# The opening and closing steps of a two-layer graph network in another order, with x of pair 3 loaded ahead of the later weights

## The reference

```
def gat_heads(x, adj, W, a):
    Wh = einsum('bnf,hfo->bhno', x, W)
    f1, f2 = Wh @ a[:, :O], Wh @ a[:, O:]
    e = leaky(f1[..., :, None] + f2[..., None, :])
    attn = softmax(where(adj > 0, e, -1e9), axis=-1)
    return einsum('bhnm,bhmo->bhno', attn, Wh)

h = relu(layernorm(x))
h = elu(gat_heads(h, adj, W_heads, a_heads))            # 4 heads
out = elu(gat_heads(concat_heads(h), adj, W_out, a_out))
y = relu(out @ w1 + b1) @ w2 + b2 + out
x = x + layernorm(y) * gamma + beta
h = relu(layernorm(x))
x = x + deg * (h @ Wi + b) + adj @ (h @ Wj)
```

## Time and profile before

| | us |
|---|---|
| median of 3 runs | 864.49 |
| lowest and highest | 864.18 and 865.11 |
| the profiled execution | 865.5 |
| its span, from first to last instruction | 863.5 |
| its mean granted TensorE clock | 0.992 |

### The profile page before, as it was taken

How to read it: one execution, slowest core, us unless ns; L and a number is a source line. 1 busy time by engine, 2 the same in 40 slices (tenths; PEclk the granted TensorE clock), 3 DMA queues, 4 the chain that set the end, 5 groups by cost and what they waited for, 6 DMA issues and landing times.

```text
span 863.5 us, 20301 instructions
## 1 busy us (share of the span) xinstructions
PE 848.3 (98%) x6389; PEld 786.7 (91%) x6389; DVE 691.9 (80%) x1984; ACT 668.2 (77%) x1802; POOL 688.6 (80%) x933
## 2 busy tenths in 40 slices
PE   7899999999999999999999999999999999999987
PEld 6699999999999999999999999999999999999974
DVE  1677888888888888888888888888888888878677
ACT  4588888788788787878878787887878788877652
POOL 1468888888888888888888888888888888798773
PEclk9699999999999999999999999999999999999999
DMA  7200001111100111110111111011111001000001
GB/s 286 74 13 16 29 9 37 38 38 38 38 11 29 38 38 38 38 38 4 35 38 38 38 38 38 2 38 38 38 38 38 27 12 39 25 25 27 5 34 37
DMA packets 15513, 32.38 MB, mean 37 GB/s; under 512 B 1840, under 2 KB 2224, under 8 KB 15024
## 3 DMA queue, kind: packets, MB, share of 16 engines
q1 hardware_dynamic: 15120, 30.94, 11.0%
q10 hardware_dynamic: 288, 0.14, 0.1%
HBM read 22.69 MB, written 8.39 MB: 36 GB/s over the span
## 4 chain that ended last, share of the span: by engine, by line
PE 92%; DVE 2%; DMA 2%; POOL 1%; issue 1%; ACT 1%; SPq 0%; DVEq 0%; POOLq 0%; ACTq 0%
PE ps L1404 83%; PE ps L1522 3%; DMA xa<-in_x 2%; PE ps L1478 2%; PE ps L1620 2%; PE ps L1591 2%; PE ps L1544 1%; PE ps L1392 1%; POOL h_lo L437 0%; ACT h L1132 0%; DVE wo L857 0%; POOL ov_lo L459 0%; ACT h_hi L1169 0%; DVE b_st L656 0%; POOL b_rs L429 0%
## 5 line engine op out<-in xcount | busy, mean ns | idle before, releaser
L437 POOL TENSOR_TENSOR h_lo<-lend,h_hi 128x512 fp32r<-128x512 f32 x128 | 165.5, 1294 | 46.8 <-ACT h_hi L1156 46.7
L1404 PE MATMUL ps<-gh_hi,wh_hi 128*128 128x256 f32 x512 | 150.7, 294 | 0.2 <-issue 0.2
L1404 PE MATMUL ps<-wo_hi,h_hi 128*128 128x258 f32 x512 | 150.1, 293 | 0.0
L1404 PE MATMUL ps<-wo_lo,h_hi 128*128 128x258 f32 x512 | 144.9, 283 | 0.0
L1404 PE MATMUL ps<-wo_hi,h_lo 128*128 128x258 f32 x512 | 144.4, 282 | 0.0
L1404 PE MATMUL ps<-gh_hi,wh_lo 128*128 128x256 f32 x512 | 143.1, 279 | 0.0
L1404 PE MATMUL ps<-gh_lo,wh_hi 128*128 128x256 f32 x512 | 142.7, 279 | 0.0
L670 DVE TENSOR_TENSOR gh_lo<-ps,gh_hi 128x512 fp32r<-128x512 f32 x128 | 88.0, 690 | 49.4 <-ACT gh_hi L1099 49.3
L715 DVE SCALAR_TENSOR_TENSOR lend<-lend,ps 128x512 f32<-128x512 f32 x128 | 87.6, 685 | 17.5 <-POOL lend L443 16.4
L1404 PEld LDWEIGHTS ps<-wo_lo,h_hi 128*128 128x128 f32 x512 | 97.1, 190 | 3.9
L1404 PEld LDWEIGHTS ps<-wo_hi,h_hi 128*128 128x128 f32 x512 | 96.7, 189 | 4.3
(11 more groups left out here) (171 smaller groups left out, 2714.9 us busy)
## 6 DMA issues: line engine op xcount, KB each, us to landing
xa<-in_x SPq DMA_DIRECT2D x32, 256.0 KB, 3.5
xr<-in_x SPq DMA_DIRECT2D x32, 256.0 KB, 2.9
out<-res SPq DMA_DIRECT2D x31, 256.0 KB, 3.1
lend<-in_w_heads_t SPq DMA_DIRECT2D x2, 512.0 KB, 5.2
lend<-in_w_heads SPq DMA_DIRECT2D x1, 1024.0 KB, 7.9
lend<-in_w_out_t SPq DMA_DIRECT2D x1, 1024.0 KB, 5.0
wo<-in_w_out SPq DMA_DIRECT2D x1, 1024.0 KB, 7.0
rows_bc<-in_rows SPq DMA_DIRECT2D x1, 512.0 KB, 8.2
```

Of the source, the lines that this page charges most:

```text
L437: pool.tensor_tensor(h2_lo[:, u, :, :].rearrange("p c n -> p (c n)"), h2v[u % 2][:, :], h2_hi[:, u, :, :].rearrange("p c n -> p (c n)").bi ...
L1404: return pe.matmul(out_, lhs, rhs, start=start, stop=stop)
```

## The change

SP loads x of pair 3 ahead of the three later weights. `first()` and `last()` of POOL, DVE, ACT and PE are written in another order; `one()` is the same. No step is added or left out, except fillers: the opening has 34 instead of 33, and the closing part 16 instead of 18. The diff, cut to the opening and to the one end of the closing part that shows fillers:

```diff
 SP, first():
-load_x(pair(0)); load_heads_t(); load_x(pair(1)); load_heads(); load_x(pair(2)); load_out_t(); load_later_weights(); load_x(pair(3))
+load_x(pair(0)); load_heads_t(); load_x(pair(1)); load_heads(); load_x(pair(2)); load_out_t(); load_x(pair(3)); load_later_weights()
 POOL, first():
-rstd1(pair(0)); rstd1(pair(1)); h_low(pair(0)); h_low(pair(1)); rstd1(pair(2)); soft(pair(0), 0); soft(pair(0), 1); out_low()
-soft(pair(1), 0); rstd1(pair(3)); elu_less(pair(0), 0); elu_less(pair(0), 1); h2_low(pair(0), 0); soft(pair(1), 1)
+rstd1(pair(0)); rstd1(pair(1)); rstd1(pair(2)); h_low(pair(0)); soft(pair(0), 0); soft(pair(0), 1); out_low(); h_low(pair(1))
+soft(pair(1), 0); elu_less(pair(0), 0); elu_less(pair(0), 1); rstd1(pair(3)); h2_low(pair(0), 0); h2_low(pair(0), 1)
...
 ACT, first():
-row_selectors(); norm1(pair(0)); ht_copy(pair(0)); norm1(pair(1)); heads_high(); rows_copy(pair(0)); ht_copy(pair(1)); h_high(pair(0))
-h_high(pair(1)); score_leaky(pair(0), 0); soft_exp(pair(0), 0); score_leaky(pair(0), 1); norm1(pair(2)); rows_copy(pair(1))
+row_selectors(); norm1(pair(0)); ht_copy(pair(0)); norm1(pair(1)); h_high(pair(0)); heads_high(); rows_copy(pair(0)); h_high(pair(1))
+score_leaky(pair(0), 0); ht_copy(pair(1)); soft_exp(pair(0), 0); score_leaky(pair(0), 1); norm1(pair(2)); rows_copy(pair(1))
 soft_exp(pair(0), 1); at_high(pair(0), 0); out_high(); at_high(pair(0), 1); score_leaky(pair(1), 0); gh_high(pair(0), 0)
-gh_high(pair(0), 1); soft_exp(pair(1), 0); gh_high(pair(0), 2); gh_high(pair(0), 3); out_scores_high(); score_leaky(pair(1), 1)
-l1w_high(); ht_copy(pair(2)); elu_exp(pair(0), 0); soft_exp(pair(1), 1); elu_exp(pair(0), 1); h2_high(pair(0), 0); at_high(pair(1), 0)
+gh_high(pair(0), 1); soft_exp(pair(1), 0); gh_high(pair(0), 2); gh_high(pair(0), 3); ht_copy(pair(2)); l1w_high()
+score_leaky(pair(1), 1); out_scores_high(); h_high(pair(2)); elu_exp(pair(0), 0); elu_exp(pair(0), 1); soft_exp(pair(1), 1)
...
 PE, first():
-warm(8, 0); heads_products(0); heads_products(1); h_transposes(pair(0)); heads_products(2); heads_products(3); score_cols(pair(0))
-h_transposes(pair(1)); warm(2, 0); score_rows(pair(0)); warm(2, 0); scores(pair(0), 0); out_products(0); warm(2, 0)
-scores(pair(0), 1); out_products(1); score_cols(pair(1)); out_products(2); score_rows(pair(1)); out_products(3); warm(2, 0)
-scores(pair(1), 0); prob_transposes(pair(0), 0); warm(9, 0); prob_transposes(pair(0), 1); gh_unit(pair(0), 0); gh_unit(pair(0), 1)
-scores(pair(1), 1); warm(4, 3); gh_unit(pair(0), 2); gh_unit(pair(0), 3); h_transposes(pair(2)); warm(4, 3); h2_unit(pair(0), 0, 0)
+warm(9, 0); heads_products(0); heads_products(1); heads_products(2); h_transposes(pair(0)); heads_products(3); score_cols(pair(0))
+warm(4, 0); score_rows(pair(0)); h_transposes(pair(1)); scores(pair(0), 0); warm(5, 0); scores(pair(0), 1); out_products(0)
+score_cols(pair(1)); warm(4, 0); score_rows(pair(1)); out_products(1); prob_transposes(pair(0), 0); scores(pair(1), 0)
+out_products(2); out_products(3); warm(4, 0); prob_transposes(pair(0), 1); gh_unit(pair(0), 0); gh_unit(pair(0), 1)
+scores(pair(1), 1); h_transposes(pair(2)); warm(2, 3); gh_unit(pair(0), 2); gh_unit(pair(0), 3); warm(6, 3); h2_unit(pair(0), 0, 0)
 h2_unit(pair(0), 0, 1); h2_unit(pair(0), 1, 0); h2_unit(pair(0), 1, 1); score_cols(pair(2)); prob_transposes(pair(1), 0)
...
 PE, last():
-hidden_by_rows(pair(31), 1); gather(pair(29)); ffn_out(pair(31)); warm(2, 0); ffn_by_rows(pair(31), 0); h3_transposes(pair(30))
-ffn_by_rows(pair(31), 1); warm(2, 0); mixed(pair(30), 0); mixed(pair(30), 1); warm(3, 0); gather(pair(30)); warm(4, 0)
+gather(pair(29)); ffn_out(pair(31)); warm(2, 0); ffn_by_rows(pair(31), 0); h3_transposes(pair(30)); ffn_by_rows(pair(31), 1)
+mixed(pair(30), 0); mixed(pair(30), 1); warm(3, 0); gather(pair(30)); warm(4, 0); h3_transposes(pair(31), 0)
```

209 lines of the change are left out of this document (105 added, 104 removed).

## The result

| | before | after |
|---|---|---|
| median of the runs, us | 864.39 (4 runs) | 858.08 (4 runs) |
| lowest and highest | 864.18 and 865.11 | 856.88 and 860.59 |
| ratio to before, 95% interval | | 0.9929 [0.9905, 0.9954] |
| the profiled execution | 865.5 | 860.59 |
| its span | 863.5 | 858.5 |

The changed kernel is 6.3 us faster by these medians. The same kernel was run again later, together with the experiments: seven more executions from 853.52 to 862.34, median 860.44, ratio 0.9933 [0.9905, 0.9960]. All eleven have a median of 858.88. So one figure is uncertain by a microsecond or two, and the scatter has grown: of the 71 executions of the kernel before, 70 lie between 863.69 and 866.34. The 71st, at 1382.5 us with a mean granted clock of 0.559, is a disturbed one and is compared with nothing. Where the scatter comes from turned out to be half of the story.

What follows compares the result with a forecast made beforehand. TensorE (PE) was taken as the bound, with the gain in the opening: 2.0 + 2.5 + 1.9 - 0.2 = 6.2 us, from the median 864.5 to 858.3 us. The range was 854.6 to 862.7.

Steps and rivals of the forecast that it cites:

- Part 1: Opening: earlier DVE statistics and third heads_products ahead of the transposes end PE's wait for h; gain 2.0 us.
- part 2: Opening: earlier load of x of pair 3 and earlier score_mask remove the wait for masked scores; gain 2.5 us.
- part 3: PE's list from the first masked scores to the first h2_unit, its length set by the clock; gain 1.9 us.
- The first of the two branches: Opening: clock rises near 21, falls at about 24.4, returns at 34.5; h2_unit at 39.1, gain 5.3 us.
- Rival 1: Opening: clock holds from 21 on, h2_unit at 35.0, gain 9.4 us, time 855.1; chance 0.27.
- Rival 2: Opening: clock does not rise near 21, h2_unit at 42.3, gain 2.1 us, time 862.4; chance 0.17.
- Rival 3: Tail: a longer PE wait for ov_lo of pair 31 loses the clock, time 867.4; chance 0.06.
- part 5: Tail: same multiplications in another order, two fillers fewer; taken as 0, between -1 and +1 us.
- Rival 4: First untouched steps: ACT gives back 1 to 3 us, time 859 to 861; chance 0.50 together with the forecast.
- part 4: Other queues: h_high(2) on ACT and h_low(1) on POOL stand earlier; cost 0 to 0.6 us, taken as 0.2.

Runs made afterwards that it cites:

- the third heads_products alone: Kernel before with one edit: on PE the third heads_products moved ahead of the transposes of pair 0; 865.14 us, ratio 1.0006.
- the load undone: Changed kernel with the old load order, later weights ahead of x of pair 3; 861.11 us, ratio 0.9960.
- the start undone: Changed kernel with the old order of DVE's selectors, statistics and variances and of PE's transposes of pair 0; 859.71 us, ratio 0.9946.
- the masked scores alone: Kernel before with one edit: on DVE score_mask(0, 0) placed ahead of norm1_stats(3); 860.87 us, ratio 0.9963.
- the closing part undone: Changed kernel with the old order of last() on POOL, DVE, ACT and PE; 859.33 us, ratio 0.9933.
- more fillers: Changed kernel with eleven more fillers on PE between the small products from 21 to 31 us; 858.16 us, ratio 0.9924.
- the load alone: Kernel before with one edit: x of pair 3 loaded ahead of the later weights; 860.45 us, ratio 0.9962.
- both edits: Kernel before with x of pair 3 loaded ahead of the later weights and the third heads_products ahead of the transposes; 860.43 us, ratio 0.9948.
- the last experiment: Changed kernel with four out_products moved behind the first gh_units, replacing eight fillers there; fillers 4 and 9 take their place; 856.58 us, ratio 0.9908.
- no fillers from 15 to 24: Changed kernel without the thirteen fillers between the first score_cols and the second score_rows; 860.72 us, ratio 0.9954.

## Why the prediction was right, and where it wasn't

**Part 1, the start.** In the trace as written: transposes at 11.26 without a wait (11.2 said), heads_products done at 13.85 (13.85), no wait for the second half of the weights, the masked scores at 19.21 (19.15). What I didn't say is that this gain depends on part 2. Alone it is worth nothing (the third heads_products alone, ratio 1.0006). On top of the load it is worth 0.7 to 1.8 us, and undone in the changed kernel 0.8, with intervals too wide to tell it from 0 or from 2. The 2.0 us are shown as a moment in a trace and not as a median. DVE's part of the start was tried only together with PE's: in the two traces with PE's order alone the transposes wait 0.20 and 0.23 us for `h`, so with a slow opening it is worth no more than that.

**Part 2, x of pair 3.** This is the larger part of the gain and was priced too low. 2.5 us was the idle time; the edits alone gave 3.9 and 3.5, because without the idle time the products behind it run in part at full clock. I had put that second share into part 3, as if it belonged to the new list of PE; it came with the old list too. The sentence "Either edit alone removes the wait" holds with the old start and fails with the new one: with the load undone PE waits 2.63 us. Its 2.2 us in the median have intervals that overlap. w_out was issued at 14.36 (14.3 said), and out_high stood directly behind at_high, at 27.56.

**Part 3, the list by the clock.** The first of the two branches is this trace, nearly to the tenth: rise near 21.0 (near 21), fall at 24.40 (24.4), gh_unit at 33.00 (33.2), clock back at 34.64 (34.5), h2_unit at 39.46 (39.1). The value I took, the middle between two branches, was 1.4 us too high for it (6.4 us up to h2_unit, 4.98 measured): in this execution PE's list is hardly shorter than in before (4.38 of the 4.98 us are the two waits). It gained 4.9 us against its counterpart of before and not 6.2. That the median of four still came out at 858.08 against 858.3 said is in part the luck of these four, since seven others gave 860.44 and all eleven 858.88. The step that failed is the one that treated the clock as one unknown with one answer. It is answered anew in each execution: 24 products took 5.1 us in one trace and 3.0 in the other.

**Rival 1, the clock holds.** It exists. In the trace of the start undone the clock held from 21.6 on, with the same list behind the first scores, and h2_unit came at 37.05 with a start 2.4 us late; less these, 34.7, where I had said 35.0. The executions of 853.52 and 854.62 are where such an opening would end (855.1 said), but neither was profiled. Their mean granted clock is 0.994 in both, so about ten us at half clock are on record in each (an estimate: twice 0.006 of 852 us); a fall did happen, and that it came early, as in the trace of the start undone (7.99, held from 21.6), fits the time but isn't shown. **Rival 2, no rise**: one of eleven, at 862.34, stands at the 862.4 said, again without a trace. Its mean clock of 0.992 has a fall on record too, as in before (0.992, half from 24.39 to 38.03), where a clock that stays down until its rise prints 1.000, as with the third heads_products alone. So a fall with a late return explains it as well, and rival 2 is not shown. **Rival 3, the tail, and part 5:** the order of last() is worth nothing, and 819.0 us lie behind h2_unit with either. **Rival 4 and part 4:** nothing is given back behind h2_unit, since its gain of 4.98 arrives whole at the end.

The range, 854.6 to 862.7, was meant for the unknown branch, and it is about the range over which single executions scatter: ten of eleven are inside.

**Why the scatter has grown.** With the old start an early high clock is lost again before it helps. In the traces of the masked scores alone and of the start undone sixteen products took 1.92 us, yet the transposes stand at 11.50 and 11.92, behind waits of 3.55 and 4.18 us for `h`; before has them at 11.54 with slow products. Before then holds the masked scores until 23.64 for x, and the third heads_products alone until 23.63. In the changed kernel neither moment holds PE, and what the early clock gives arrives: transposes at 9.42 instead of 11.26, everything to 22.4 by 1.9 us. This is read from traces and wasn't tried by itself, and it is a part only, for the start undone still scatters from 857.7 to 863.7.

The Trainium skill, page "TensorE: Matmul & The Clock Gate", Part 1, also says that the moment of the change differs from run to run, depending on how the kernel's start falls. The two traces of the changed kernel agree (24 products in 5.11 and in 2.99 us). The same page puts the cost of the ramp under 1% of a typical kernel's span and advises against fitting it to a count; here the executions of one program lie 1% apart (8.8 of 858.9 us), which is more than the change is worth. Its rule that activity releases the clock does not by itself describe the kernel with fillers between all products: busy from 1.86, and at half clock until 24.4 in the profiled execution.

**What stays open.** Why the clock holds behind one list in one execution and falls in another. Idle time of PE does not tell. The clock fell within 0.4 us behind a short wait for the split columns in three traces (24.40 and 22.42 in the changed kernel's two, 24.86 with the closing part undone), and in a wait in three (24.39 in before, 24.76 with more fillers, 7.99 with the start undone). It also fell amid or right behind two-column products with PE busy for two us or more: at 24.91 (the load alone), 24.99 (the masked scores alone), 23.55 (both edits), between 8.1 and 9.1 behind the early high clock of four traces, and at 32.95 in the last experiment. The second half of the changed list (POOL's and ACT's orders, score_cols and the small edits) was not tried by itself.

## What to carry to other kernels

An idle gap of the bounding engine in a place with a throttled clock can cost more than its length; here removing 2.5 us of it gained 3.5 to 3.9. An edit that makes an engine earlier is worth little while a fixed moment, such as a load's landing, stands behind it, so test such edits together with the one that moves that moment, not one by one. Where the time of single executions scatters by more than the change is worth, don't judge by one trace or four times: lay the groups of executions side by side, and look for a form that depends less on the luck (the last experiment spreads over 5.4 us, the changed kernel over 8.8), as by moving small products (two columns, 0.21 us each at half clock) from the place where PE is the late one to a place where they take what fillers had.

## What the runs showed of the hardware

- Behind the same eight or nine fillers, from 1.86 us on, the clock rose ahead of or during the first heads_products in some executions and not in others: of thirteen traces (the changed kernel and twelve experiments) six ran the first 16 or 24 of these products at 0.12 to 0.14 us each, the others at 0.22.
- TensorE was busy for 22.4 of 22.5 us, from 1.86 to 24.4, at half clock by its durations, with fillers between all small products (59% of the busy time).
- The clock fell without idle time of PE, behind 24 two-column products at full clock (the last experiment, 32.95), and amid such products behind other work in the traces of the load alone (24.91), the masked scores alone (24.99) and both edits (23.55).
- The granted clock prints as 1.00 until the first fall on record, whatever the durations say (1.00, and 1.7 us for four fillers, in the kernel with fillers between all small products).
- The last two stores, 128 KB each, landed in 1.8 us by the median in eleven of the fourteen traces and in 2.3, 2.6 and 2.9 in the other three (the third heads_products alone, the last experiment, no fillers from 15 to 24). In the last of these it moved the end of the span by 1.9 us. DMA issues of the changed kernel, and of the one without fillers from 15 to 24:

```profile
out<-res SPq DMA_DIRECT2D x2, 128.0 KB, 1.8
```

```profile
out<-res SPq DMA_DIRECT2D x2, 128.0 KB, 2.9
```
